# All gate and up products first, hidden values kept in DRAM, then all down products

## The chip, the cores and the metric

The kernel runs on one core of a Trainium2 chip. The time is the device time of the program in microseconds (us). Three timed runs of the kernel before gave 1355.43, 1355.92 and 1358.1 us, median 1355.92 us. The engines are named as the profile names them: PE (matmul), PEld (its weight load), DVE (vector), ACT (scalar), POOL (GpSimd) and SP (the queue that issues the DMAs).

## The reference, cut to what matters

```python
mod = (_silu(c) @ wmod).reshape(2, 6, 1, -1)          # shift, scale, gate of both halves
h = _layernorm(x) * (1 + ca) + sa                     # x: 2 batches x 2048 rows x 512
q, k, v = h @ q_w.T + q_b, h @ k_w.T + k_b, h @ v_w.T + v_b
qp, kp = elu(q) + 1, elu(k) + 1                       # 16 heads of 32
kv = einsum('bhsd,bhse->bhde', kp, v)
z = einsum('bhsd,bhd->bhs', qp, kp.sum(axis=2))
x = x + ga * ((einsum('bhsd,bhde->bhse', qp, kv) / (z + 1e-6)) @ o_w.T + o_b)
h = _layernorm(x) * (1 + cb) + sb
gate, up = h @ lut[gate_idx].T, h @ lut[up_idx].T     # 512 -> 1376; lut has 16 values
x = x + gb * ((silu(gate) * up) @ lut[down_idx].T)    # 1376 -> 512
```

All is float32. The kernel splits each operand of its large products into two float16 halves and makes three float16 matmuls of one float32 product (`three`, L1067 to L1075).

## The kernel before, in words

The 4096 rows are 8 groups of 512. Phase A takes the groups one after another: layer norm, transposes, 12 projections of 12 matmuls each (`out_a`: 4 of K, 4 of V, 4 of Q), the sum of the attention matrix (`kv_a`), and it stores the positive queries in DRAM. Phase B has 8 stages. Stage g makes the feed-forward half of group g and, between its pieces, the attention output of group g + 1.

The inner size of 1376 is 11 chunks `j` (the last has 96 rows). One item of phase B is one chunk of one group: gate product (12 matmuls), up product (12), then `silu(gate) * up` on ACT (L646) and DVE (`hid_full`, L1003), the split into halves on ACT (`hid_hi`, L652) and POOL (`hid_lo`, L485), and the down product (12 matmuls, 4 tiles of 3), which adds up in four PSUM banks over the 11 items. Gate and up have one PSUM bank each, so `up` of an item waits for `hid_full` of the item before.

The attention of group g + 1 goes through every engine. On PE: four `z_piece` (L1169, one in each of items 0 to 3), four `o_piece` (12 matmuls each; the first stands behind `up` and `down` of item 4), four `t_piece` (transposes, items 8 and 9). On DVE: after `hid_full` of items 0 to 3 one `qn_full` (reciprocal L941, product L943); then four `x1_tile` (L951 to L958). `o_piece(n, 0)` waits until `qn_lo` of POOL has ended for all four chunks (`qn_done`). POOL also adds the bias (`xob`, L430) between `qn_lo` 2 and 3.

The weights come as indices and are looked up by DVE (`look_step`, L807 to L830): a piece is 128 x 512 words and takes 19 steps (4 that take bits apart, 8 leaves L826, 7 picks L829). Two pieces at once make a wide unit, with the same 19 steps on 1024 words. There are 33 pieces (11 chunks x gate, up, down). Before, 29 of them are looked up in phase A, in stages of 5, 7, 7 (two groups each), 4, 3 and 3, and the last 4 in the first stage of phase B. A call of `lookup` spreads its steps over the slots of a stage; the order of each engine is the order in which the code is written. PE, DVE, ACT and POOL run the equal stages in hardware loops (`Fori`).

Of the kernel before, what the change touches and what calls it, by code (L numbers as in the profile page):

```python
# [34 lines left out]
P = 128  # L35
# [20 lines left out]
PARTS = 3  # L56
PIECES = FC * PARTS
LOOK_0, LOOK_PAIR, LOOK_5, LOOK_6, LOOK_7 = 5, 7, 4, 3, 3
LOOK_A = LOOK_0 + 2 * LOOK_PAIR + LOOK_5 + LOOK_6 + LOOK_7
LOOK_B0 = PIECES - LOOK_A  # L60

# [18 lines left out]
def adaln_kernel(nc, x, qwT, qb, kwT, kb, vwT, vb, owT, ob, lut, gateT, upT, downT, cT, wmod, out):  # L80
    with ExitStack() as ctx:
# [1270 lines left out]
```

## Time and profile before

| | |
|---|---|
| median of 3 runs | 1355.92 us |
| the profiled execution | 1356.93 us, of which the span is 1355.2 us |
| PE busy | 1203.5 us (89%) |
| DVE busy | 766.9 us (57%) |
| ACT, POOL busy | 422.2 us, 337.1 us |
| TensorE clock granted, mean | 0.951 |
| DMA | 63.86 MB, mean 47 GB/s |

The shares are averages over stages with different limits: phase A ends at about 521 us, and the rows by stage below keep them apart. A matmul's duration in the trace is longer than its distance from the next, since matmuls overlap; what a product costs is read from the starts.

### The profile page before, as it was taken

What the parts mean: (1) busy time and instruction counts of PE and PEld (TensorE: products, weight loads), DVE (VectorE), ACT (ScalarE), POOL (GpSimd) and SP (SyncE); (2) the same over time, 40 slices, a digit from 0 to 9 for tenths busy, and PEclk for the clock granted to TensorE, in tenths of its full rate; (3) what the DMA queues carried; (4) which work ended last, traced back from release to release, by engine and by line L of the source; (5) the groups of instructions that cost most, each with busy time, mean ns of one, the idle gap of its engine ahead of it and who ended that gap; (6) DMA issues with size and microseconds to landing.
All of it is one profiled execution on the core that took longest, in us unless ns stands there. A gap on an engine that the chain in (4) does not pass through costs nothing.

```text
span 1355.2 us, 14765 instructions
## 1 busy us (share of the span) xinstructions
PE 1203.5 (89%) x5464; PEld 582.6 (43%) x5464; DVE 766.9 (57%) x1073; ACT 422.2 (31%) x664; POOL 337.1 (25%) x338
## 2 busy tenths in 40 slices
PE   4587889978876757899999999999999999999998
PEld 4253345534433423344444444444444444444443
DVE  2479999999999766985833630531531531531111
ACT  0224446645534414113213213213213213212111
POOL 1120100000001013432522424324334334333212
PEclk9888899989988877899999999999999999999999
DMA  9225110111020102000200100100100100100000
GB/s 329 90 72 164 63 62 28 35 62 62 1 94 23 39 0 94 32 1 0 94 31 1 63 32 0 63 32 1 63 31 0 62 32 0 62 0 1 31 0 31
DMA packets 35455, 63.86 MB, mean 47 GB/s; under 512 B 3296, under 2 KB 13536, under 8 KB 33344
## 3 DMA queue, kind: packets, MB, share of 16 engines
q1 hardware_dynamic: 35392, 63.00, 13.7%
q8 instruction: 42, 0.69, 0.2%
q14 instruction: 21, 0.17, 0.0%
HBM read 46.22 MB, written 16.78 MB: 46 GB/s over the span
## 4 chain that ended last, share of the span: by engine, by line
PE 57%; DVE 29%; issue 9%; ACT 2%; POOL 2%; DMA 0%; POOLq 0%; ACTq 0%; DVEq 0%; SPq 0%
PE bank L1072 18%; PE bank L1073 18%; PE bank L1074 18%; DVE look_buf L829 6%; DVE look_buf L826 4%; DVE w_ffn L829 4%; PE bank L1169 2%; DVE arena L826 1%; DVE qn_f L941 1%; DVE shared L851 1%; DVE qp L859 1%; DVE look_buf L821 1%; DVE h L863 1%; PE bank L1080 1%; DVE shared L855 1%
## 5 line engine op out<-in xcount | busy, mean ns | idle before, releaser
L1072 PE MATMUL bank<-h,w_ffn 128*128 128x512 f16 (+1 forms) x704 | 269.2, 382 | 14.4 <-DVE hid_f L1003 6.1
L1074 PE MATMUL bank<-h,w_ffn 128*128 128x512 f16 (+1 forms) x704 | 269.3, 383 | 0.0
L1073 PE MATMUL bank<-h,w_ffn 128*128 128x512 f16 (+1 forms) x704 | 269.1, 382 | 0.0
L1003 DVE SCALAR_TENSOR_TENSOR hid_f<-bank,sc,shared 128x512 f32<-128x512 f32 (+1 forms) x88 | 65.9, 749 | 315.9 <-PE bank L1074 297.2
L485 POOL TENSOR_TENSOR shared<-hid_f,shared 128x512 f16<-128x512 f32 (+1 forms) x88 | 102.2, 1161 | 395.3 <-ACT shared L652 395.0
L646 ACT ACTIVATE shared<-bank,sc 128x512 f32<-128x512 f32 (+1 forms) x88 | 60.4, 686 | 273.2 <-PE bank L1074 273.2
L652 ACT ACTIVATE shared<-hid_f 128x512 f16<-128x512 f32 (+1 forms) x88 | 55.5, 631 | 281.9 <-DVE hid_f L1003 281.6
L1072 PE MATMUL bank<-w_ffn,shared 128*128 128x512 f16 (+1 forms) x352 | 137.1, 389 | 2.6 <-POOL shared L485 2.5
L1073 PE MATMUL bank<-w_ffn,shared 128*128 128x512 f16 (+1 forms) x352 | 137.0, 389 | 0.0
L1074 PE MATMUL bank<-w_ffn,shared 128*128 128x512 f16 (+1 forms) x352 | 136.6, 388 | 0.0
L1072 PE MATMUL bank<-arena,h 128*128 128x512 f16 x256 | 103.2, 403 | 12.6 <-DVE h L863 6.4
L1072 PEld LDWEIGHTS bank<-h,w_ffn 128*128 128x128 f16 (+1 forms) x704 | 71.0, 101 | 99.2 <-issue 14.9
L1073 PEld LDWEIGHTS bank<-h,w_ffn 128*128 128x128 f16 (+1 forms) x704 | 71.0, 101 | 86.4 <-issue 12.3
L941 DVE RECIPROCAL qn_f<-qn_f 128x512 f32<-128x512 f32 x32 | 107.0, 3343 | 1.8 <-ACT qn_f L598 1.8
L1074 PEld LDWEIGHTS bank<-h,w_ffn 128*128 128x128 f16 (+1 forms) x704 | 71.0, 101 | 82.9 <-issue 2.6
L1073 PE MATMUL bank<-arena,h 128*128 128x512 f16 x256 | 102.4, 400 | 0.0
L1074 PE MATMUL bank<-arena,h 128*128 128x512 f16 x256 | 101.5, 396 | 0.0
L1120 PE MATMUL bank<-shared 128*128 128x129 f32 x256 | 40.9, 309 | 50.9 <-DVE shared L855 50.9
L951 DVE SCALAR_TENSOR_TENSOR xg<-bank,sc,xg 128x512 f32<-128x512 f32 x32 | 24.0, 749 | 107.0 <-PE bank L1074 107.0
L396 POOL TENSOR_SCALAR ve<-mv 128x4 f32<-128x4 f32 x16 | 5.2, 326 | 315.8 <-DVE mv L739 211.4
L424 POOL TENSOR_TENSOR qn<-qn_f,qn 128x512 f16<-128x512 f32 x32 | 37.6, 1175 | 141.8 <-ACT qn L604 141.8
L526 ACT ACTIVATE h<-bank,modm 128x512 f16<-128x512 f32 x64 | 49.4, 773 | 53.6 <-PE bank L1080 27.6
(162 smaller groups left out, 1897.4 us busy)
## 6 DMA issues: line engine op xcount, KB each, us to landing
xg<-in_x SPq DMA_DIRECT2D x16, 1024.0 KB, 6.6
qp_dram<-qp SPq DMA_DIRECT2D x8, 1024.0 KB, 4.8
qp<-qp_dram SPq DMA_DIRECT2D x7, 1024.0 KB, 4.8
out<-xg SPq DMA_DIRECT2D x7, 1024.0 KB, 4.3
w_ffn<-in_wmod SPq DMA_DIRECT2D x5, 1024.0 KB, 14.3
w_ffn<-in_gateT SPq DMA_DIRECT2D x10, 256.0 KB, 4.5
w_ffn<-in_upT SPq DMA_DIRECT2D x10, 256.0 KB, 4.7
w_ffn<-in_downT SPq DMA_DIRECT2D x10, 256.0 KB, 5.1
```

What stands on the lines that cost most here:

```text
L485: pool.tensor_tensor(hid[0:m, i, 1], hid_f[0:m, i], hid[0:m, i, 0], ALU.subtract).then_inc(hid_done, 1)
L526: act.activation(h[:, par, 0, c], bank[c % 2][:], ACT.Identity, bias=bias, scale=scale)
L646: act.activation(silu_g[0:m, j % 2], bank[6][0:m], ACT.Silu, scale=c1(C_INV_G)[0:m]).then_inc(silu_g_done, 1)
L652: act.activation(hid[0:m, i, 0], hid_f[0:m, i], ACT.Copy).then_inc(hid_hi_done, 1)
L826: ins = dve.tensor_scalar(buf(dst), buf("m0"), tab_x[:, a:a + 1], tab[:, 2 * a:2 * a + 1], ALU.bitwise_and, ALU.bitwise_xor)
L829: ins = dve.copy_predicated(buf(dst), buf(a), buf(b))
L941: dve.reciprocal(qn_f[:, c % 2], qn_f[:, c % 2]).then_inc(rec_done, 1)
L1003: dve.scalar_tensor_tensor(hid_f[0:m, i], bank[7][0:m], c1(C_HID)[0:m], silu_g[0:m, i], ALU.mult, ALU.mult).then_inc(hid_f_done, 1)
L1072: pe.matmul(dst, a_hi, b_hi, start=first, stop=False)
L1073: pe.matmul(dst, a_hi, b_lo, start=False, stop=False)
L1074: last = pe.matmul(dst, a_lo, b_hi, start=False, stop=end)
L1120: last = pe.matmul(bank[6 + c // 2][:, at:at + n], kp[:, t % 2, c * P:(c + 1) * P], v_one[:, t % 2, c], start=(t == 0 and c % 2 == 0), sto ...
```

## The change: what it does, and the diff

- Phase B makes gate and up products only. The split hidden values of each item go to DRAM (`hid_dram`, 256 KB an item), through three buffers (`HIDS = 3`). A third phase C loads them group by group (two buffers of 11 chunks, laid over the gate and up weights, which are done with by then) and makes all down products, 33 items of three matmuls in one PSUM bank after the other. The rows `x` after attention go to DRAM (`x1_dram`) and come back in phase C.
- Gate and up have two PSUM banks each, so an item waits for the one two items back. The normed rows have three buffers (`H2S = 3`).
- The lookup goes in the order gate and up of all chunks, then down. Phase A does 16 pieces: one wide unit in each of groups 0 to 5, two single pieces in groups 6 and 7. Phase B does 17 single pieces: three in each of stages 0 to 4, two in stage 5. Stages 0, 1, 2 have 9, 11 and 13 items, since chunks 9 and 10 of groups 0 and 1 wait for their weights; the others have 11, and the last stage has no attention.
- The first stage of phase B has the attention pieces one or two items earlier than the others.
- The loops are written out.

```diff
-LOOK_0, LOOK_PAIR, LOOK_5, LOOK_6, LOOK_7 = 5, 7, 4, 3, 3
+HIDS = 3
+H2S = 3
+LOOK_A = [[(0, True)], [(2, True)], [(4, True)], [(6, True)], [(8, True)], [(10, True)],
+          [(12, False), (13, False)], [(14, False), (15, False)]]
+LOOK_B = [[(p, False) for p in range(a, b)] for a, b in ((16, 19), (19, 22), (22, 25), (25, 28), (28, 31), (31, PIECES))]
+HELD = FC - 2
+STAGES = [[(0, j) for j in range(HELD)],
+          [(1, j) for j in range(HELD)] + [(0, j) for j in range(HELD, FC)],
+          [(1, j) for j in range(HELD, FC)] + [(2, j) for j in range(FC)]]
+STAGES += [[(g, j) for j in range(FC)] for g in range(3, BATCHES * SEQ // GROUP)]
...
+            def hid_load(g):
+                par = g % 2
+                for s, count in landed(SLOT[(g, FC - 1)]):
+                    sp.wait_ge(s, count)
+                sp.dma_start(hid_all[par][:, 0:FC - 1]..., hid_dram[g][:, 0:FC - 1]).then_inc(hid_in[par], 16)
...
+                    sp.wait_ge(hid_done, e + 1)
+                    sp.dma_start(hid_dram[g][0:m, j], hid[0:m, e % HIDS]...).then_inc(hid_out[e % HIDS], 16)
...
             def hid_hi(e, j):
+                if e >= HIDS:
+                    act.wait_ge(hid_out[e % HIDS], 16 * (e // HIDS))
...
+                units = LOOK_B[s] if s < len(LOOK_B) else None
+                shares = HELD if s < 2 else len(STAGES[s])
+                for i, (g, j) in enumerate(STAGES[s]):
+                    if n < GROUPS:
+                        run(before, i)
+                    run(early, i)
+                    hid_full(SLOT[(g, j)], j)
+                    if n < GROUPS:
+                        run(after, i)
+                    run(extra, i)
+                    if units and i < shares:
+                        lookup(units, i, shares)
...
-                    up(g, par, j)
-                    if j:
-                        down(g, j - 1)
+            def up(g, j):
+                e = SLOT[(g, j)]
+                if e >= 2:
+                    pe.wait_ge(hid_f_done, e - 1)
+                gate_up(g, j, 1, bank[3 + 2 * (e % 2)]).then_inc(up_done, 1)
+
+            def down(g, t):
+                par, k = g % 2, 4 * g + t
+                if t == 0:
+                    pe.wait_ge(hid_in[par], 32 * (g // 2 + 1))
+                pe.wait_ge(y_read, k + 1)
+                ...
+                three(bank[2 + t][:], pairs).then_inc(sum_done, 1)
...
+            for s in range(2, GROUPS):
+                stage_b(s)
+            pe.wait_ge(hid_f_done, GROUPS * FC)
+            pe.wait_ge(down_ready, 1)
+            for g in range(GROUPS):
+                for t in range(TILES):
+                    down(g, t)
```

On DVE, one of the equal stages of phase B, items 0 to 3. Before:

```order
L1003 SCALAR_TENSOR_TENSOR hid_f<-bank,sc,shared 128x512
L941 RECIPROCAL qn_f<-qn_f 128x512
L943 SCALAR_TENSOR_TENSOR qn_f<-qp,qn_f 128x512
L1003 SCALAR_TENSOR_TENSOR hid_f<-bank,sc,shared 128x512
L941 RECIPROCAL qn_f<-qn_f 128x512
```

On DVE of the changed kernel, the same place in stage 3 (L1053 is `hid_full`, L994 and L996 `qn_full`, L878 to L886 lookup steps), from item 1 on:

```order
L1053 SCALAR_TENSOR_TENSOR hid_f<-bank,sc,shared 128x512
L994 RECIPROCAL qn_f<-qn_f 128x512
L996 SCALAR_TENSOR_TENSOR qn_f<-qp,qn_f 128x512
L883 TENSOR_SCALAR w_ffn<-look_buf,tab_x,tab 128x512
L883 TENSOR_SCALAR look_buf<-look_buf,tab_x,tab 128x512 x2
L886 COPY_PREDICATED w_ffn<-look_buf 128x512
L886 COPY_PREDICATED look_buf<-look_buf 128x512
L1053 SCALAR_TENSOR_TENSOR hid_f<-bank,sc,shared 128x512
L994 RECIPROCAL qn_f<-qn_f 128x512
L996 SCALAR_TENSOR_TENSOR qn_f<-qp,qn_f 128x512
```

Five lookup steps now stand between the product of one item and `hid_full` of the next.

On SP, one stage of phase B. Before (queries, output rows, input rows):

```order
L339 DMA qp<-qp_dram 128x2048
L346 DMA out<-xg 128x4x512
L349 DMA xg<-in_x 128x4x512
L353 DMA look_buf<-in_owT 128x4x512
L339 DMA qp<-qp_dram 128x2048
```

On SP of the changed kernel, one stage of phase B with its 11 stores of hidden values (L398):

```order
L369 DMA qp<-qp_dram 128x2048
L398 DMA hid_dram<-shared 128x1024 x3
L357 DMA x_dram<-xg 128x2048
L398 DMA hid_dram<-shared 128x1024 x2
L363 DMA xg<-in_x 128x4x512
L398 DMA hid_dram<-shared 128x1024
L398 DMA hid_dram<-shared 96x1024
L398 DMA hid_dram<-shared 128x1024 x4
L369 DMA qp<-qp_dram 128x2048
```

The store of the output has moved to phase C; the stores of hidden values and of `x` are new.

## Rows read from the trace of the kernel before

**Rows 1.** The page: busy time by engine; one group (busy us, mean ns | idle before)

```profile
PE 1203.5 (89%) x5464; PEld 582.6 (43%) x5464; DVE 766.9 (57%) x1073; ACT 422.2 (31%) x664; POOL 337.1 (25%) x338
...
L424 POOL TENSOR_TENSOR qn<-qn_f,qn 128x512 f16<-128x512 f32 x32 | 37.6, 1175 | 141.8 <-ACT qn L604 141.8
```

**Rows 2.** Busy time in windows, one a stage (columns are named in its first row)

```profile
core 0: us, PE busy (x) PEld busy (x) DVE busy (x) ACT busy (x) POOL busy (x), PEclk, DMA share, GB/s
73.70:140.70 67.00, 53.66 (x264) 31.23 (x263) 59.09 (x97) 27.50 (x43) 7.21 (x6) 0.90 0.42 119
140.70:192.00 51.30, 44.91 (x211) 22.82 (x210) 48.27 (x66) 25.92 (x41) 5.24 (x4) 0.90 0.12 42
192.00:233.70 41.70, 35.00 (x175) 18.97 (x174) 40.41 (x65) 24.45 (x39) 2.54 (x4) 0.92 0.15 51
...
323.70:378.10 54.40, 45.22 (x224) 23.39 (x222) 53.38 (x82) 25.84 (x41) 2.29 (x4) 0.97 0.12 39
378.10:437.60 59.50, 42.57 (x188) 21.68 (x188) 57.08 (x105) 25.13 (x40) 8.52 (x9) 0.86 0.15 53
437.60:521.40 83.80, 50.11 (x213) 24.66 (x214) 61.47 (x90) 31.13 (x51) 17.64 (x16) 0.78 0.17 63
521.40:636.90 115.50, 106.11 (x456) 47.59 (x457) 92.24 (x125) 28.25 (x44) 37.12 (x31) 0.94 0.03 10
636.90:747.40 110.50, 108.02 (x482) 49.50 (x481) 52.11 (x66) 26.75 (x42) 37.37 (x37) 0.98 0.11 39
...
849.70:952.00 102.30, 102.30 (x469) 47.10 (x468) 34.22 (x35) 26.76 (x42) 36.38 (x36) 1.00 0.09 32
...
1156.70:1259.00 102.30, 102.30 (x469) 47.13 (x468) 34.22 (x35) 24.31 (x38) 36.44 (x36) 1.00 0.06 21
```

**Rows 3.** Groups on DVE, 140.7 to 233.7 us: wide and single lookup steps

```profile
L829 DVE COPY_PREDICATED look_buf<-qn,arena 128x1024 uint32<-128x1024 uint32 x9 | 12.3, 1364 | 0.1
L826 DVE TENSOR_SCALAR look_buf<-arena,tab_x,tab 128x1024 uint32<-128x1024 uint32 x12 | 9.8, 816 | 0.1
...
L826 DVE TENSOR_SCALAR look_buf<-look_buf,tab_x,tab 128x512 uint32<-128x512 uint32 x7 | 3.6, 536 | 0.0
L829 DVE COPY_PREDICATED look_buf<-look_buf 128x512 uint32<-128x512 uint32 x4 | 3.0, 742 | 0.1
```

**Rows 4.** Timeline of PE in a full stage (start us, us, what)

```profile
952.02 0.38 PE L1072 MATMUL bank<-h,w_ffn 128*128 128x512 f16 x1
...
954.61 0.39 PE L1072 MATMUL bank<-w_ffn,shared 96*128 96x512 f16 x1
...
957.33 1.02 PE L1169 MATMUL bank<-qp,same_head 128*128 128x512 f32 x2
...
994.91 0.38 PE L1072 MATMUL bank<-arena,qn 128*128 x1
```

**Rows 5.** Timeline of DVE in the same stage, item 2

```profile
975.85 0.75 DVE L1003 SCALAR_TENSOR_TENSOR hid_f<-bank,sc,shared 128x512 f32<-128x512 f32 x1 [4.01 <-PE bank L1074]
...
979.89 0.69 DVE L943 SCALAR_TENSOR_TENSOR qn_f<-qp,qn_f 128x512 f32<-128x512 f32 x1
```

**Rows 6.** Timelines of DVE, POOL and PE in the first stage of phase B

```profile
555.25 1.81 DVE L829 COPY_PREDICATED w_ffn<-look_buf 128x512 uint32<-128x512 uint32 x1
...
558.64 2.88 DVE L826 TENSOR_SCALAR look_buf<-look_buf,tab_x,tab 128x512 uint32<-128x512 uint32 x2
...
555.00 6.23 POOL L430 TENSOR_TENSOR xg<-xg,obga 128x512 f32<-128x512 f32 x4
...
564.48 0.61 PE L1072 MATMUL bank<-h,w_ffn 128*128 128x512 f16 x1 [6.14 <-DVE hid_f L1003]
...
569.58 0.45 PE L1072 MATMUL bank<-w_ffn,shared 128*128 128x512 f16 x1
```

**Rows 7.** DMA issues: out<-in, KB each, us to landing

```profile
qp_dram<-qp SPq DMA_DIRECT2D x8, 1024.0 KB, 4.8
...
out<-xg SPq DMA_DIRECT2D x4, 256.0 KB, 2.0
```

More of the change, by code:

```diff
@@ L479, in _ @@
             for c in range(KC):
[L480 to L498 removed]
+                h_lo_b(0, c)
@@ L499, in stage_b, with m1_max @@
+            def m1_max():
+                pool.wait_ge(h2_done, 4 * 2 + 4 + 1)
+                all_max(S_M1, 8)
+            for s in range(GROUPS):
+                stage_b(s, {8: [m1_max]} if s == 1 else {})
+            for g in range(GROUPS):
+                par = g % 2
+                pool.wait_ge(x1_in[par], 16 * (g // 2 + 1))
                 for t in range(TILES):
@@ L830, in look_step, with lookup, looked @@
                 ins.then_inc(look, 1)
-            def in_twos(first, pieces):
-                return [(first + p, p + 1 < pieces) for p in range(0, pieces, 2)]
-            def lookup(units, before, share, shares):
-                total = len(units) * STEPS
-                if share == 0:
-                    dve.wait_ge(look, before)
-                    dve.sem_clear(look)
+            def lookup(units, share, shares):
+                first, total = UNITS.index(units[0]), len(units) * STEPS
                 for i in range(total * share // shares, total * (share + 1) // shares):
                     p, wide = units[i // STEPS]
-                    look_step(p, wide, i % STEPS, i // STEPS * STEPS)
+                    look_step(p, wide, i % STEPS, (first + i // STEPS) * STEPS)
+            def looked(unit, ready):
+                dve.wait_ge(look, (UNITS.index(unit) + 1) * STEPS)
+                dve.sem_inc(ready, 1)
             def k_bias(g, t):
@@ L870, in kv_sum, with stage_a @@
                     dve.tensor_tensor(acc, acc, kv_bank[i], ALU.add).then_inc(kv_read, 1)
-            def stage_a(g, par, more, look=None, extra={}, late=0):
+            def stage_a(g, par, more, units=None, extra={}, late=0):
                 if more:
@@ L887, in stage_a @@
                         kv_sum(g)
-                    if look:
-                        units, before, share, shares = look
-                        lookup(units, before, share + o, shares)
+                    if units:
+                        lookup(units, o, OUTS)
                 qp_sum(g, KC - 1)
@@ L983, in look_7 @@
                 for share in shares:
-                    lookup([(first_6 + LOOK_6 + p, False) for p in range(LOOK_7)], LOOK_6 * STEPS, share, OUTS)
+                    lookup(LOOK_A[7], share, OUTS)
             stage_a(7, 1, False, extra={
@@ L1007, in y_tile @@
                 k = 4 * g + t + 1
+                dve.wait_ge(sum_done, k)
                 dve.wait_ge(y_done, k + 2)
```

512 lines of the change are left out of this document (253 added, 259 removed).

## The prediction, made before the changed kernel had run

> **What bounds the kernel now.** First the page: PE is busy for 89% of the span, DVE for 57% [rows 1]. These are means over two kinds of stage, so next the windows by stage [rows 2]. In phase A (to 521.4 us) DVE is busy nearly always, 48.27 of 51.30 us or 40.41 of 41.70, and PE is not: DVE, with its lookups, sets the pace. From 849.7 us on a stage takes 102.3 us and PE is busy in all of it, DVE in 34.22: PE sets the pace. Last the timelines, for what a piece costs on each engine and how long the attention's way through DVE is.
>
> **PE's work in phases B and C.** The starts 952.02, 954.61 and 957.33 give 12 matmuls of a gate or up product 2.59 us and 12 of a down product 2.72 [rows 4]. A full stage is 11 x (5.18 + 2.72) = 86.9, so the attention's pieces on PE take 102.3 - 86.9 = 15.4. The change moves the down products and drops none: 88 x 7.90 + 7 x 15.4 = 803.0 us before and after. A stage of 11 items without down is 57.0 + 15.4 = 72.4 us; those of 9 and 13 items are 62.0 and 82.7.
>
> **Phase A: lookups leave DVE.** A wide step of the two common kinds takes 1.364 or 0.816 us, a single one 0.742 or 0.536 [rows 3]. Four bit steps (my estimate: 0.7 wide, 0.42 single), 8 leaves and 7 picks, less some 0.09 of overlap a step, make 17.2 us for a wide unit and 9.5 for a single piece. Group 0 loses one wide unit and a single one: 26.7 us of DVE. Groups 1 and 3 go from two wide units to one (17.2), 2 and 4 from a wide and a single one to one wide (9.4), 5 loses 17.2, 6 and 7 lose 9.5 each. That is 116 us, but PE's own work catches up: 12 projections of 2.59, the attention matrix and the transposes are some 36.5 us a group, and the last query sum of a group, the statistics and the first key product of the next stand in a row over three engines. I take 39.5 us for groups 1 to 4 (the 41.70 us stage, which has 40.41 of DVE work, is the nearest row; the floor is 36.5). So: group 0 from 67.0 to 53 (PE's columns and rows of the modulation stay), groups 1 to 4 from 183.0 to 158, group 5 from 54.4 to 41, group 6 from 59.5 to 50.5 (it stays DVE's: 57.08 busy), group 7 from 83.8 to 77, since its chain of reciprocals hardly has lookups in it [rows 2]. Sum: **68 us less**; bounds 45 (the chain over three engines holds each group at 43) and 82 (PE's floor everywhere).
>
> **Phase B: the attention's way no longer fits.** This is the term that decides. The first `o_piece` starts 994.91 - 952.02 = 42.9 us into a stage [rows 4], and five down products stand before it. Without them PE is there at 42.9 - 13.6 = 29.3 us. It needs all four chunks of `qn_full` and their halves. On DVE `hid_full` and `qn_full` of an item take 975.85 to 980.58, 4.7 us, and DVE waited 4.01 us for PE before it: DVE had room [rows 5]. Without lookups the fourth `hid_full` can start at 24.3 (four items of 5.18 and four of 0.86 on PE), its product ends at 29.0, the halves on POOL, 1.175 [rows 1], and on ACT, some 0.7 by the DVE product of that size [rows 5], end at 31: 2 us late. That is stage 6. In stages 3 and 4 three pieces are spread over 11 items, 5 steps behind each product, as the order of DVE shows. The chain is 6.1 (first `up`) + 3 x 4.7 + 15 steps (7.1) + 4.7 = 32.0, and what POOL costs.
>
> What POOL costs: in the first stage of phase B a single pick takes 1.81 us beside `xob` where it takes 0.742 alone, two leaves 2.88 instead of 1.0, and `xob` itself 6.23 [rows 6]. `qn_lo` and `xob` fall into just the three shares that count. I take 4.3 us a stage (a step held up by some 0.9 us twice, and two or three in the third share); bounds 1 and 8. The product then ends at 36.3, the halves at 38.3: PE waits 9 us. After a wait of this kind PE ran slowly: from 564.48 the 12 matmuls behind a wait of 6.14 us took 5.1 us to 569.58, at half the clock [rows 6], 2.5 us more. With 0.7 for the second chain (x1, norm, `t_piece`), which also has fewer PE products beside it, a stage loses 12.
>
> The Trainium skill has a rule on this in "SBUF — State Buffer", section "Who interferes with whom": DVE operations in a two-port mode or with two SBUF inputs and GpSimd operations exclude each other for a whole instruction, and the later one is fully blocked. By that rule all three pieces' steps of a stage are exposed to each of POOL's 31 operations, which speaks against moving them out of phase A, where POOL is nearly idle. The 1.81 us of the row agree with it. By it alone the loss of a stage would be nearer my upper bound, 8 us of POOL's cost, and the whole, with 3.7 more in six stages, near 1394 us.
>
> Stage by stage, what PE loses: stage 0 has 6.3 steps a share and its chain begins one item earlier, where PE is at 26: 15 of waiting, 2.5 of clock, and at the end the clamps of three rows and the last lookup stand before the halves of the next group, 5.5: 23. Stage 1 has 6.3 steps and the second attention matrix, for which DVE was busy 52.11 instead of 34.22 us [rows 2], partly in the chain, and POOL's maximum, for which DVE waits: 25. Stage 2, with what DVE brings along from there, 4.4 steps: 18. Stages 3 and 4: 12 each. Stage 5, two pieces, 3.5 steps: 10. Stage 6: 4. Stage 7: nothing. Together 104.
>
> Before, phase B took 1355.2 - 521.4 = 833.8, so 30.8 more than 803.0. Of these I keep 4 for the second matrix's products on PE and 4 for the end (last rows on DVE and POOL, and a DMA of 2.0 us [rows 7]); 23 go, and 104 + 1.5 (PE turns to phase C) come: **82.5 us more**. Two-deep banks are in this: they let PE run two items ahead of `hid_full`, but nothing lets it pass `o_piece`.
>
> **DRAM.** A store of 256 KB lands in 2.0 us, 1024 KB in 4.8 [rows 7]. The ring of three gives a store two items, 10 us: hidden, even behind a 1 MB transfer. A group's 2.75 MB in phase C need by the same row some 13 us, with output and input of 1 MB 23, beside 11 x 2.72 = 29.9 us of PE: hidden. The first load has the last four items (21 us) of stage 7. If loads ran at half that rate, phase C would show 16 us for each of six groups. Nothing there, 0 to 96 as bounds, with nearly all weight at 0.
>
> **Loops.** A stage in a loop and the last full one outside take 102.30 us alike [rows 2]: nothing. The Trainium skill ("Runtime: NRT & Kernel Launch", "Instruction fetch mechanics") says that a taken branch can stop the fetch and recommends unrolling; by it there would be a gain, which these two rows do not show.
>
> **Sum.** 1355.2 - 68 + 82.5 = 1369.7 of span, 1371.4 with the 1.7 us around it. The median of the runs is 1.0 under the profiled execution: 1370.5, rounded for the many small lags that were left out to **1372 us**.
>
> **Rivals.** (1) *Faster: the attention's way hides.* If POOL's operations fall beside the reciprocals, which do not use what lookups use, and DVE's queue is not in step with the items, stages 2 to 5 lose some 5 us, stages 0 and 1 some 12. Then 48 come instead of 104: 1316. For it speaks that DVE as a whole has time (34 + 29 of 72 us); against it that the shares stand before the next reciprocal in the same queue. (2) *Slower by much: DVE becomes the bound of stages 0 to 5.* In the first stage four pieces and a share raised DVE's busy time to 92.24 us. If a piece costs 13 us with POOL beside it, three make 39 and DVE's stage is 71 to 90 us with waits on top: stages lose 5 more each, 1400. It decides from some 12 us a piece. (3) *Slower: phase C waits for its loads,* 8 us for each of six groups on top of my forecast: 1420. Rows 7 speak against it. (4) *Phase A gains less,* 45: 1395; the 41.70 us stage speaks against it, since it is only 1.3 us longer than DVE's work. *Little changes:* the two terms are equal, within 3 us: only by accident.
>
> **Numbers.** A measurement of this kernel can tell 0.2%, 2.7 us, from no change. Forecast (1350 to 1392) 0.55, rival 1 0.22, rival 2 0.12, rival 3 0.03, rival 4 0.08. Of the forecast's own spread some 0.03 lies within 2.7 us of the time before and 0.02 below it, and rival 1 reaches up to it with 0.02: faster 0.22, same 0.05, slower 0.73. The range is 1328 to 1402; the likeliest case's own is 1352 to 1392.
>
> **What would show it.** Right: the first projections of phase B start at about 453 us; stages 1 to 4 of phase A take 38 to 41 us; in stages 2 to 5 of phase B the first matmul of `o_piece` has an idle time of 6 to 15 us in front of it, put down to POOL's `qn`, and half the clock behind it; phase C has PE busy throughout, 239 us. Wrong: stages 3 and 4 at 76 us or less, or waits in front of a group's first down product.

## The result, and the profile after

The changed kernel takes 1389.8 us (median of 4 runs, 1387.4 to 1391.8) against 1356.3 (4 runs, 1355.4 to 1358.1): ratio 1.0233, 95% interval 1.0214 to 1.0253. It is 33.5 us slower where 16 were forecast. The profiled execution took 1390.5 us, its span 1388.7. First the page, for [rows 1] and [rows 7]: busy time by engine, and DMA issues.

```profile
PE 1209.4 (87%) x5464; PEld 581.3 (42%) x5464; DVE 829.2 (60%) x1149; ACT 424.0 (31%) x664; POOL 356.8 (26%) x339
...
hid_dram<-shared SPq DMA_DIRECT2D x80, 256.0 KB, 2.0
w_ffn<-hid_dram SPq DMA_DIRECT2D x8, 2560.0 KB, 9.6
```

TensorE does the same 5464 matmuls; its busy time grows by 5.9 us (1203.5 before), since more of them run at the lower clock. The other 27.6 of the 33.5 us by which the span grew are idle time of TensorE. The windows tell where; for [rows 2], groups 0, 1, 2, 5 and 6 with 7 of phase A, then stages 0 to 7 of phase B and phase C.

```profile
72.20:126.20 54.00, 51.84 (x258) 30.58 (x257) 33.34 (x58) 27.27 (x43) 4.87 (x7) 0.87 0.46 138
126.20:170.60 44.40, 39.74 (x194) 20.77 (x193) 31.20 (x47) 25.41 (x40) 2.52 (x4) 0.92 0.14 48
170.60:207.10 36.50, 36.50 (x193) 19.69 (x192) 30.94 (x46) 25.41 (x40) 2.22 (x4) 1.00 0.17 58
280.20:322.50 42.30, 40.34 (x212) 21.66 (x211) 36.64 (x62) 25.95 (x41) 2.19 (x4) 1.00 0.15 51
322.50:455.00 132.50, 94.96 (x416) 47.91 (x414) 103.69 (x160) 56.55 (x91) 26.06 (x25) 0.84 0.18 62
...
455.10:543.00 87.90, 67.06 (x289) 30.12 (x290) 72.54 (x92) 25.40 (x40) 34.05 (x29) 0.89 0.28 102
543.00:655.50 112.50, 83.37 (x348) 38.28 (x349) 87.09 (x123) 26.07 (x41) 33.35 (x31) 0.85 0.15 52
655.50:753.20 97.70, 86.56 (x385) 40.44 (x384) 72.90 (x92) 29.45 (x46) 40.19 (x33) 0.95 0.18 64
753.20:839.70 86.50, 75.40 (x338) 34.84 (x337) 71.61 (x87) 26.70 (x42) 36.77 (x31) 0.94 0.21 72
839.70:927.20 87.50, 76.46 (x336) 35.19 (x336) 72.54 (x89) 26.69 (x42) 37.37 (x31) 0.94 0.19 69
927.20:1009.20 82.00, 74.96 (x336) 34.75 (x336) 59.91 (x72) 26.93 (x42) 36.32 (x31) 0.96 0.20 73
1009.20:1087.20 78.00, 74.37 (x337) 34.68 (x337) 34.12 (x35) 24.69 (x38) 31.97 (x31) 0.98 0.18 64
1087.20:1145.30 58.10, 57.20 (x266) 26.39 (x265) 9.00 (x12) 14.57 (x23) 12.71 (x11) 1.00 0.26 98
1145.30:1388.70 243.40, 238.78 (x1056) 100.88 (x1056) 24.02 (x32) 0.58 (x1) 42.11 (x33) 0.99 0.40 143
```

Phase A gives what it should: phase B starts at 455.1 instead of 521.4 us, 66.3 less. Groups 2 to 4 take 36.5 us, and PE is busy in all of it. Phases B and C take 933.6 instead of 833.8 us, 99.8 more, and C has no part in it: 243.4 us, PE busy for 238.8. Against the lengths of the prediction (62.0, 72.4, 82.7, four times 72.4, 57.0) the stages of B lose 25.8, 40.2, 15.0, 14.0, 15.1, 9.6, 5.6 and 1.0 us, 126.3 together; stage 1's contains some 4 us of the second M's products. "Lost" means this difference below.

Timeline of PE, stage 3, for the last of [rows 4] (start us, us, what [idle before <-releaser]):

```profile
791.10 0.59 PE L1116 MATMUL bank<-arena,qn 128*128 128x512 f16 x1 [8.36 <-issue]
...
795.96 0.38 PE L1116 MATMUL bank<-h,w_ffn 128*128 128x512 f16 x1
```

TensorE waits 8.36 us in front of the first `o_piece`, and its 12 matmuls take 4.86 us instead of 2.59. DVE's timeline, and then POOL's, say what it waits for, though the row names no engine ("issue"):

```profile
781.96 1.40 DVE L883 TENSOR_SCALAR look_buf<-look_buf,tab_x,tab 128x512 uint32<-128x512 uint32 x1
783.27 0.74 DVE L1053 SCALAR_TENSOR_TENSOR hid_f<-bank,sc,shared 128x512 f32<-128x512 f32 x1
783.94 3.34 DVE L994 RECIPROCAL qn_f<-qn_f 128x512 f32<-128x512 f32 x1
787.31 1.38 DVE L996 SCALAR_TENSOR_TENSOR qn_f<-qp,qn_f 128x512 f32<-128x512 f32 x1
```

POOL at the same time:

```profile
780.64 2.43 POOL L480 TENSOR_TENSOR qn<-qn_f,qn 128x512 f16<-128x512 f32 x1 [2.83 <-ACT qn L660]
783.03 5.11 POOL L486 TENSOR_TENSOR xg<-xg,obga 128x512 f32<-128x512 f32 x4
788.10 1.60 POOL L540 TENSOR_TENSOR shared<-hid_f,shared 128x512 f16<-128x512 f32 x1
789.66 1.33 POOL L480 TENSOR_TENSOR qn<-qn_f,qn 128x512 f16<-128x512 f32 x1
```

The fourth product ends at 788.69, 35.5 us into the stage (forecast 36.3), its low half on POOL at 790.99, and PE starts at 791.10. This is the forecast's mechanism.

Stage 1 has this wait too, 17.64 us, the longest of the phase. Behind it comes another, which was not forecast. Both on PE:

```profile
591.88 0.58 PE L1116 MATMUL bank<-arena,qn 128*128 128x512 f16 x1 [17.64 <-issue]
...
648.29 0.66 PE L1116 MATMUL bank<-h,w_ffn 128*96 128x512 f16 x1 [11.48 <-DVEq L899]
```

Then DVE, up to that moment:

```profile
630.72 0.77 DVE L1053 SCALAR_TENSOR_TENSOR hid_f<-bank,sc,shared 128x512 f32<-128x512 f32 x1
642.74 0.15 DVE L750 TENSOR_SCALAR sc<-sc 128x1 f32<-128x1 f32 x1 [11.25 <-POOL sc L446]
...
643.68 0.73 DVE L886 COPY_PREDICATED w_ffn<-look_buf 128x512 uint32<-128x512 uint32 x1
...
647.45 0.73 DVE L886 COPY_PREDICATED w_ffn<-look_buf 128x512 uint32<-128x512 uint32 x1
```

And POOL:

```profile
633.34 1.16 POOL L498 TENSOR_TENSOR arena<-h_f,arena 128x512 f16<-128x512 f32 x1
642.33 0.38 POOL L446 PARTITION_ALL_REDUCE sc<-sc  x1 [7.82 <-issue]
649.45 1.14 POOL L498 TENSOR_TENSOR arena<-h_f,arena 128x512 f16<-128x512 f32 x1 [6.75 <-issue]
```

DVE stands at `m_scale(1)` (L750) for 11.25 us, until POOL's maximum over the partitions is there. From the end of its operation before, POOL takes 8.2 us to it (7.82 put down to issue, 0.38 to the instruction), and 6.75 us more pass until its next operation, a low half of the next group's normed rows (L498, `h_lo_b`). Behind `m_scale` in DVE's queue stands the last share of stage 1's lookups, which completes piece 21, and gate (0,10) waits for that piece (L899 is `looked`). So TensorE waits for GpSimd's reduction, through a lookup that has nothing to do with it. DVE stood at the same place before the change, where it held nobody up (L693 is the same scale there):

```profile
733.71 0.15 DVE L693 TENSOR_SCALAR sc<-sc 128x1 f32<-128x1 f32 x1 [9.39 <-POOL sc L390]
```

### The profile page after: what moved, and what is told of

Its sections match the earlier page's. It is cut to its first block, busy times and chain, and to the rows that moved or that the text cites. A ratio compares the mean times of both kernels' runs of the same rounds, so it can differ in the third digit from the quotient of the medians.

```text
span 1388.7 us, 14324 instructions
## 1 busy us (share of the span) xinstructions
PE 1209.4 (87%) x5464; PEld 581.3 (42%) x5464; DVE 829.2 (60%) x1149; ACT 424.0 (31%) x664; POOL 356.8 (26%) x339
## 3 DMA queue, kind: packets, MB, share of 16 engines
q1 hardware_dynamic: 52160, 124.87, 25.8%
## 4 chain that ended last, share of the span: by engine, by line
PE 53%; issue 11%; DVE 6%; POOL 4%; ACT 1%; DMA 0%; POOLq 0%; DVEq 0%; SPq 0%; ACTq 0%
PE bank L1116 17%; PE bank L1117 16%; PE bank L1118 16%; PE bank L1213 2%; DVE look_buf L883 2%; POOL arena L493 1%; DVE look_buf L886 1%; POOL shared L540 1%; DVE w_ffn L886 1%; DVE hid_f L1053 1%; PE bank L1124 1%; PE bank L1203 0%; DMA h<-qp_dram 0%; POOL rstd L454 0%; PE bank L1164 0%
## 5 line engine op out<-in xcount | busy, mean ns | idle before, releaser
L1116 PE MATMUL bank<-h,w_ffn 128*128 128x512 f16 (+1 forms) x528 | 204.0, 386 | 23.8 <-DVEq L899 17.1
L1117 PE MATMUL bank<-h,w_ffn 128*128 128x512 f16 (+1 forms) x528 | 203.8, 386 | 0.0
L1118 PE MATMUL bank<-h,w_ffn 128*128 128x512 f16 (+1 forms) x528 | 203.2, 385 | 0.0
L540 POOL TENSOR_TENSOR shared<-hid_f,shared 128x512 f16<-128x512 f32 (+1 forms) x88 | 110.2, 1252 | 340.1 <-ACT shared L708 340.1
L1060 DVE SCALAR_TENSOR_TENSOR shared<-bank,sc,gb_row 128x512 f32<-128x512 f32 x32 | 24.0, 751 | 215.6 <-PE bank L1118 215.6
L1053 DVE SCALAR_TENSOR_TENSOR hid_f<-bank,sc,shared 128x512 f32<-128x512 f32 (+1 forms) x88 | 65.8, 748 | 138.3 <-PE bank L1118 106.5
L1116 PE MATMUL bank<-w_ffn 128*128 128x512 f16 (+1 forms) x352 | 136.3, 387 | 0.9 <-DVE hid_f L1053 0.9
L1117 PE MATMUL bank<-w_ffn 128*128 128x512 f16 (+1 forms) x352 | 136.2, 387 | 0.0
L1118 PE MATMUL bank<-w_ffn 128*128 128x512 f16 (+1 forms) x352 | 136.2, 387 | 0.0
L1116 PE MATMUL bank<-arena,qn 128*128 128x512 f16 x128 | 54.7, 427 | 74.6 <-issue 74.6
L1116 PE MATMUL bank<-arena,h 128*128 128x512 f16 x256 | 102.1, 399 | 11.5 <-issue 7.0
L883 DVE TENSOR_SCALAR look_buf<-look_buf,tab_x,tab 128x512 uint32<-128x512 uint32 x147 | 109.6, 777 | 0.8
L994 DVE RECIPROCAL qn_f<-qn_f 128x512 f32<-128x512 f32 x32 | 107.0, 3344 | 4.2 <-ACT qn_f L654 4.2
L701 ACT ACTIVATE shared<-bank,sc 128x512 f32<-128x512 f32 (+1 forms) x88 | 60.3, 685 | 115.2 <-PE bank L1118 115.1
L571 POOL TENSOR_TENSOR xg<-xg,shared 128x512 f32<-128x512 f32 x32 | 41.0, 1280 | 198.1 <-DVE shared L1060 198.1
L1116 PEld LDWEIGHTS bank<-h,w_ffn 128*128 128x128 f16 (+1 forms) x528 | 53.7, 102 | 89.0 <-issue 15.4
L1117 PEld LDWEIGHTS bank<-h,w_ffn 128*128 128x128 f16 (+1 forms) x528 | 53.7, 102 | 65.5 <-issue 11.3
L1118 PEld LDWEIGHTS bank<-h,w_ffn 128*128 128x128 f16 (+1 forms) x528 | 53.8, 102 | 63.4 <-issue 4.0
L480 POOL TENSOR_TENSOR qn<-qn_f,qn 128x512 f16<-128x512 f32 x32 | 45.6, 1424 | 120.3 <-ACT qn L660 120.3
## 6 DMA issues: line engine op xcount, KB each, us to landing
out<-xg SPq DMA_DIRECT2D x7, 1024.0 KB, 11.2
```

What stands on the lines that cost most here:

```text
L480: pool.tensor_tensor(qn[:, 1, c], qn_f[:, c % 2], qn[:, 0, c], ALU.subtract).then_inc(qn_done, 1)
L540: pool.tensor_tensor(hid[0:m, e % HIDS, 1], hid_f[0:m, e % 2], hid[0:m, e % HIDS, 0], ALU.subtract).then_inc(hid_done, 1)
L571: pool.tensor_tensor(xg[:, par, t], xg[:, par, t], y_t[:, t % 2], ALU.add).then_inc(y_done, 1)
L701: act.activation(silu_g[0:m, e % 2], bank[2 + 2 * (e % 2)][0:m], ACT.Silu, scale=c1(C_INV_G)[0:m]).then_inc(silu_g_done, 1)
L883: ins = dve.tensor_scalar(buf(dst), buf("m0"), tab_x[:, a:a + 1], tab[:, 2 * a:2 * a + 1], ALU.bitwise_and, ALU.bitwise_xor)
L994: dve.reciprocal(qn_f[:, c % 2], qn_f[:, c % 2]).then_inc(rec_done, 1)
```

## The experiments

Eleven kernels ran, each timed beside the kernel before; a ratio is to that one. The changed kernel is called "after" here. The kernel before took 1357.0 us beside experiments 1 to 4, 1358.0 beside 5 to 8 and 1360.2 beside 9 to 11, which ran on another chip than 1 to 8. Differences in microseconds to after, or between these sets, carry that drift of up to 4 us; the lengths of stages inside one execution do not. Two stages of the same code still differ by up to some 2.5 us: stage 0, whose program is that of after, lost 25.8 us there and 28.2 in experiment 4.

**1. No lookups in phase B.**

```
-                    if units and i < shares:
-                        lookup(units, i, shares)
...
-                            looked((p, False), gu_ready)
+                            dve.sem_inc(gu_ready, 1)
...
```

> The changed kernel without the 17 lookups of phase B (the weights of these pieces stay raw indices). Theory A (the lookups stand on DVE ahead of the reciprocals, and PE waits for them at the first o_piece): each of the stages 2 to 5 loses what stage 6 loses now, 5.6 us, instead of 15.0, 14.0, 15.1 and 9.6; stage 0 loses some 12 instead of 25.8, stage 1 some 16 instead of 40.2. Together 1390 - 69 = 1321 us. Theory B (with the down products gone the attention's way is too long for the stage even without lookups): waits of 6 to 8 us stay at each o_piece, 1355 us or more. Theory C (the traffic with DRAM holds phase B up): 1380 to 1390 us, no stage much shorter.

Measured 1333.2 us (ratio 0.981, 0.977 to 0.986): the lookups cost 56.6 us. The stages lose 13.2, 28.1, 7.1, 4.1, 5.8, 5.8, 5.8 and 1.0 us. Work is left out here, so 1333.2 is no time that a whole kernel could reach by this. The expected 1321 was missed by 12 us. Stage 1 loses 28.1 even so, and each later stage to stage 6 keeps a wait of 3.2 us in front of `o_piece`, where 2 had been worked out for stage 6:

```profile
751.75 0.38 PE L1114 MATMUL bank<-arena,qn 128*128 128x512 f16 x1 [3.19 <-issue]
```

In stage 1, 8.6 us of waiting are left at `o_piece` and 6.5 at gate (0,10). The second is the wait for POOL's maximum again: the signal that stands for piece 21 is still given behind `m_scale(1)`.

**2. All lookups, none of them beside the reciprocals.**

```
+                    first = 2 if s == 0 else 3
+                    k, parts = i - first, shares - first
+                    if units and 0 <= k < parts:
+                        lookup(units, k, parts)
...
```

> The same lookups, all of them, but in a stage's items 3 and later (2 and later in stage 0), behind the fourth reciprocal, none before. Theory A: the waits at o_piece shrink to some 3 us (as in stage 6) and stages 2 to 5 lose 6 to 8 us each instead of 13.4 in the mean; stage 0 gives back 8, stage 1 few, since its last share still stands behind POOL's maximum: 1350 to 1358 us. Rival (DVE's load as such is the bound, 34 us and three pieces in 72): the wait moves to the second half of the stage, before the transposes, and the time stays within 10 us of 1390.

Measured 1367.5 us (ratio 1.006, 1.003 to 1.008), 22 less than after with the same work. Stages 3 and 4 in windows:

```profile
742.40:824.50 82.10, 74.75 (x338) 34.73 (x337) 68.39 (x84) 26.85 (x42) 37.13 (x31) 0.98 0.20 74
824.50:906.60 82.10, 74.73 (x336) 34.74 (x336) 70.83 (x89) 26.53 (x42) 37.27 (x31) 0.98 0.20 73
```

DVE is nearly as busy as in after (68.4 and 70.8 us against 71.6 and 72.5) and the stages are 4 to 5 us shorter: of the 56.6 us that the lookups of phase B cost, some 22 are the price of where they stand. The other 34 stay, so their amount costs too. The waits at `o_piece` fall to 3.6 us (3.2 without lookups), and `t_piece` now waits 3.1 us for POOL's rows. The expected 1350 to 1358 was missed. Stage 0 gave back 2 us and not 8: `o_piece` waits 5.5 us instead of 11.9, but a gate now waits 2.6 us for its lookup, and the wait at the end grew from 6.6 to 7.8; stages 3 and 4 lost 9.7 and 9.8, not 6 to 8; and stage 1 gained 1.4 (38.8 us lost), for its wait for piece 21 grew to 13.6 us. The rival, a time within 10 us of 1390, is rejected too.

**3. `xob` at the start of a stage instead of in the chain.**

```
-                              3: [lambda: qn_lo(n, 2), lambda: xob(n, par)],
+                    before = {0: [lambda: xob(n, par)], ...
```

> Only POOL's adding of the bias (xob, four operations, 5.1 us) is moved in stages 1 to 6 from item 3 to item 0, where DVE waits for the first up product. Theory A with a share for POOL: the third lookup share is no longer held up and qn_lo(3) no longer stands behind xob, 1.5 to 3 us less in each of the six stages: 1373 to 1381 us. Rival (POOL's operations cost the lookups nothing that counts): 1390 us.

Measured 1395.8 us (ratio 1.027, 1.023 to 1.031): a miss, 6 us worse than after. Stage 1 loses 3.3 less, stages 2 to 5 lose 1.0 to 3.4 more each. `xob` now meets the share that the last item of the stage before left. DVE at the start of stage 3:

```profile
749.96 6.50 DVE L886 COPY_PREDICATED look_buf<-look_buf 128x512 uint32<-128x512 uint32 x1
756.49 0.73 DVE L886 COPY_PREDICATED look_buf<-look_buf 128x512 uint32<-128x512 uint32 x1
757.26 0.74 DVE L886 COPY_PREDICATED w_ffn<-look_buf 128x512 uint32<-128x512 uint32 x1
757.89 0.74 DVE L1053 SCALAR_TENSOR_TENSOR hid_f<-bank,sc,shared 128x512 f32<-128x512 f32 x1
```

POOL there:

```profile
749.76 1.19 POOL L540 TENSOR_TENSOR shared<-hid_f,shared 96x512 f16<-96x512 f32 x1 [2.77 <-ACT shared L708]
750.90 4.95 POOL L486 TENSOR_TENSOR xg<-xg,obga 128x512 f32<-128x512 f32 x4
```

One pick, 0.73 us alone like the one behind it, took 6.50 beside POOL's four additions, and the first reciprocal started 10.5 us into the stage. The contention is shown and is worse than forecast where it falls on a pick; the place for `xob` was wrong. The Trainium skill ("SBUF — State Buffer", "Who interferes with whom") has the later operation blocked for a whole instruction; here the pick, which had started 0.2 us after POOL's first operation in the rows (L540), ended only at 756.46, behind that operation and the whole run of four, which ended at 755.85.

**4. `m_scale(1)` one item later.**

```
-                        8: [lambda: m_scale(1)], 9: [lambda: m_cut(1, 0), lambda: m_cut(1, 1)],
+                        9: [lambda: m_scale(1), lambda: m_cut(1, 0)],
...
```

> Only the scale and the first cut of the second attention matrix are moved behind DVE's last lookup share of stage 1 (item 9 instead of 8). Theory D (the 11.5 us in which PE waits for gate product (0, 10) come from the last share of piece 21, which stands on DVE behind the wait for POOL's maximum): this wait goes, 8 to 11 us less, 1379 to 1382 us. Rival (DVE is late in stage 1 anyway): the wait turns up in stage 2 instead, and 3 us or less are won.

Measured 1386.8 us (ratio 1.020, 1.017 to 1.024), 3 us less: the wait goes, as theory D has it, but the time is the rival's. The wait of gate (0,10) falls from 11.5 to 0.9 us and stage 1 loses 26.6 instead of 40.2; stage 2 loses 26.0 instead of 15.0. The two stages together lose 52.6 instead of 55.2. So the cause of the wait is shown, and taking it away by itself wins little. Stage 2 takes it back in two places. Its first `o_piece` waits 13.4 us instead of 8.4, since the scale and the cuts now stand at the stages' border, and a new wait of 4.2 us comes near its start, which experiment 5 has too.

**5. M's scale and cuts in stage 2.**

```
-                        8: [lambda: m_scale(1)], 9: [lambda: m_cut(1, 0), lambda: m_cut(1, 1)],
-                        10: [lambda: m_cut(1, 2), lambda: m_cut(1, 3), lambda: dve.sem_inc(m_ready, 1)]},
+                stage_b(s, {8: [lambda: m_scale(1)], 9: [lambda: m_cut(1, 0)], 10: [lambda: m_cut(1, 1)],
+                            11: [lambda: m_cut(1, 2)], 12: [lambda: m_cut(1, 3), ...]} if s == 2 else {})
```

> The changed kernel with VectorE's scale and four cuts of the second batch's M moved out of stage 1 (items 8 to 10) into stage 2 (items 8 to 12); POOL's maximum stays where it is, and M is wanted only in stage 3. Nothing else moves. The theory that VectorE's queue stood behind the wait for POOL's maximum, and the lookup shares behind it: the wait of gate (0,10), 11.5 us, goes, and since neither scale nor cuts stand in stage 1 any more, stage 2 does not take it over as it did in the run with the scale one item later: stage 1 loses 24 to 29 us instead of 40.2, stage 2 stays at 14 to 17, and the time is 1374 to 1380 us. The rival, that the sum of VectorE's work in stages 1 and 2 decides and not the wait inside it (the cuts alone are some 8 us): stage 2 loses 8 us more than now, and the time is 1383 to 1388 us.

Measured 1382.8 us (ratio 1.018, 1.013 to 1.022): 7 less by the medians, between the two and next to the rival's 1383. The profiled execution was the slowest of the four (1387.2); in it phase B is 3.5 us shorter than in after. Stages 1 and 2:

```profile
543.10:643.10 100.00, 81.40 (x349) 37.47 (x350) 81.84 (x112) 23.89 (x38) 28.60 (x27) 0.88 0.15 56
643.10:746.70 103.60, 89.40 (x385) 41.45 (x384) 74.77 (x95) 30.82 (x49) 43.28 (x37) 0.92 0.18 63
```

Stage 1 loses 27.6 (12.6 less), stage 2 20.9 (5.9 more), stage 3 17.1 (3 more: its `o_piece` waits 11.4 us, since the cuts sit just before its first reciprocal). So of the 12.6 us that stage 1 gains, 9 come back by the windows. Stage 3's part is DVE's cuts. Stage 2's is not DVE's work, for DVE idles at the border for 14.5 us. Rows of PE, ACT and POOL show another way of the same reduction:

```profile
653.38 0.63 PE L1116 MATMUL bank<-h,w_ffn 128*96 128x512 f16 x1 [4.10 <-ACT shared L701]
...
651.22 0.78 ACT L582 ACTIVATE arena<-bank,modm 128x512 f16<-128x512 f32 x1 [11.82 <-POOL arena L498]
...
649.99 1.14 POOL L498 TENSOR_TENSOR arena<-h_f,arena 128x512 f16<-128x512 f32 x1 [6.94 <-issue]
```

POOL does nothing else from 635.2 to 650.0 us around its maximum. The low half of the normed rows (L498) stands behind it, ACT's next chunk of these rows waits for that, the silu of a gate (L701) stands behind it on ACT, and TensorE waits for the silu: 4.1 us and some 2.5 of clock. In after TensorE has no such wait there; the one of 11.5 us for the lookup lay over it.

**6. Late lookups, M in stage 2, the FFN gate rows clamped in stage 7.** The edits of 2 and 5, and `clamp(gb_row...)` moved from stage 0 to the stage without attention.

> Three moves on VectorE together, nothing left out: the lookups of phase B in items 3 and later of each stage (2 and later in stage 0), the scale and cuts of the second M in stage 2, and the clamps of the two FFN gate rows in stage 7, which has no attention, instead of stage 0. If the gains add: 1367.5 us of the run with late lookups, less the 13.6 us wait that stood in its stage 1, less 4 to 6 of the 7.75 us that gate (1,0) waited at the end of stage 0: 1346 to 1352 us. If a wait behind each takes half of it over: 1354 to 1360 us.

Measured 1364.9 us (10 runs; ratio 1.004, 1.002 to 1.007), 3 less than experiment 2, which is no more than the runs of either scatter: both expectations missed. Stage 1 gains the 13.3 us (38.8 to 25.5), but stage 3 loses 17.1 instead of 9.7 and stage 2 8.7 instead of 6.0; the clamps bring 1 us, since the last half on POOL, not DVE, ends stage 0. In stage 3 three late pieces and the cuts' heap meet: DVE is busy 76.40 us of it.

**7. The attention one pair later, with pairs held back in every stage.** The kernel of 6, and from stage 2 on:

```
+STAGES += [[(g - 1, j) for j in range(HELD, FC)] + [(g, j) for j in range(HELD)] for g in range(2, ...)]
+STAGES[-1] += [(BATCHES * SEQ // GROUP - 1, j) for j in range(HELD, FC)]
...
+                    if s >= 2:
+                        b_attn = {k + (k > 4): v for k, v in b_attn.items()}
+                        a_attn = {k + 1: v for k, v in a_attn.items()}
```

and the same shift on DVE, ACT, POOL and SP.

> The kernel of the run before in this call (late lookups, M's cuts in stage 2, clamps in stage 7), and from stage 2 on each stage begins with the last two gate/up pairs of the group before and holds its own last two back (stage 7 has 13 pairs), as stages 0 and 1 do already; the attention from o_piece to h_lo_b stands one pair later in these stages. The theory that what is left in stages 2 to 6 without lookups (5.8 us each: a wait of 3.2 us at the first o_piece for the chain of four reciprocals, and what the clock loses behind it) comes from where o_piece stands: TensorE reaches it 5.2 us later, the wait goes, t_piece has the same distance from o_piece, and two pairs stand between h_lo_b and the gate that needs it. Stages 2 to 6, which lost 6.0, 9.7, 9.8, 8.4 and 5.5 us with late lookups, lose 1 to 4 each: 20 to 30 us less than the run before in this call, 1318 to 1332 us, faster than both kernels. The rival, that the waits follow (t_piece 5 us, or the stage's end): within 6 us of the run before.

Measured 1340.8 us (ratio 0.987, 0.983 to 0.992): 24 less than the kernel of 6, as expected, and faster than both kernels; the expected 1318 to 1332 was missed because that kernel was slower than thought. Stages 2 to 6 lose 5.0, 11.6, 6.8, 2.4 and 0.8 us. The wait at `o_piece` is gone in all but stage 3 (4.1 us, behind the cuts), so the rest found in experiment 1 was the place of `o_piece`. What is left in these stages is mostly waiting at the first `t_piece` for POOL's rows, 2.1 to 4.8 us in stages 2 to 5.

**8. Every hidden value stored twice.**

```
+                    sp.dma_start(hid_twin[g][0:m, j], hid[0:m, e % HIDS]...).then_inc(hid_out[e % HIDS], 16)
```

> The changed kernel with each of the 88 stores of the hidden values done twice (256 KB once more, into a second DRAM tensor; each buffer comes free only when both have landed). It doubles what the DRAM passage costs, if it costs anything: by the theory that the stores are hidden (three buffers, 2.0 us a store against 5.2 us a pair) the time is the changed kernel's within 2 us, 1388 to 1392 us. If the passage through DRAM was part of the loss, by contention of the DMA queues or by buffers that come free late, it is 1395 us or more.

Measured 1388.6 us (ratio 1.021, 1.017 to 1.026), 1.2 less than after: no price, as expected. The stages' losses are those of after within 0.2 us, and the stores still land in 2.0 and 2.4 us:

```profile
hid_twin<-shared SPq DMA_DIRECT2D x80, 256.0 KB, 2.4
```

**9. After, with its 17 lookups dealt 3, 3, 1, 1, 2, 2, 2, 3 to eight stages.**

```
-LOOK_B = ... for a, b in ((16, 19), (19, 22), (22, 25), (25, 28), (28, 31), (31, PIECES))]
+LOOK_B = ... for a, b in ((16, 19), (19, 22), (22, 23), (23, 24), (24, 26), (26, 28), (28, 30), (30, PIECES))]
```

> The changed kernel with the 17 lookups of phase B dealt 3, 3, 1, 1, 2, 2, 2, 3 to the eight stages instead of 3, 3, 3, 3, 3, 2, 0, 0; nothing left out, nothing else moved. Against the run without any, the lookups cost stages 2 to 5 now 7.9, 9.9, 9.3 (three each) and 3.8 us (two). If a stage pays only for what goes beyond its slack (two cost 3.8, one costs nothing or 1, three in stage 7, which has no attention, nothing): 7, 9 and 5.5 us less in stages 2, 3 and 4, 4 more in stage 6: some 17 us less, 1370 to 1375 us. The rival, each lookup step at the same price wherever it stands: 3.3 us a lookup, so only the three that go to stage 7 are won: 10 us less, 1378 to 1382 us; if stage 7 pays too, 1388 us.

Measured 1378.9 us (ratio 1.014, 1.011 to 1.017): 11 less by the medians, 13 by the ratios. The time lies in the rival's range; the stages decide against it. Stages 2 to 7 lose 4.9, 6.2, 9.4, 9.5, 9.5 and 5.8. For the price of a lookup stage by stage: against the run without any, one makes stage 2 shorter by 2.2 us and stage 3 longer by 2.1. Both come mostly from the clock behind `o_piece` (12 matmuls in 2.59 us against 5.07, and in 3.87 against 2.59), so one costs next to nothing; two cost 3.6 to 3.8, three 7.9 to 9.9 (stages 2 to 4 of after). The price rises, as the first expectation had it, but stage 7 was not free: the last piece stands in front of phase C, whose first matmul waits 5.6 us for it.

**10. The kernel of 7 with that deal.**

> The skewed kernel (late lookups, M's cuts in stage 2, clamps in stage 7, pairs held back in every stage) with the lookups dealt 3, 3, 1, 1, 2, 2, 2, 3. Its stages lost 5.0, 11.6, 6.8, 2.4, 0.8 and 1.0 us from stage 2 on. Stage 3 lost 4.1 us at the first o_piece behind VectorE's cuts of M and lookups, and 3.6 at the first transpose. If VectorE's backlog set these: 6 to 12 us less, 1329 to 1335 us. If not (the transposes wait for POOL's rows in any case): within 3 us of 1340.8, and stage 6 up to 2 us longer.

Measured 1332.7 us (ratio 0.979, 0.976 to 0.981), 8 us less than experiment 7 as expected, and the fastest kernel of the study. Stages 2 to 4:

```profile
639.40:713.90 74.50, 72.75 (x337) 34.46 (x336) 50.37 (x59) 27.07 (x43) 36.48 (x33) 1.00 0.22 75
713.90:788.60 74.70, 72.73 (x338) 34.49 (x337) 48.89 (x57) 26.39 (x42) 34.27 (x31) 1.00 0.23 80
788.60:863.40 74.80, 72.75 (x338) 34.48 (x337) 57.73 (x67) 26.84 (x42) 35.55 (x31) 1.00 0.23 81
```

They take 74.5 to 74.8 us where TensorE's own work is 72.4, at the full clock. What is left stands above all in stage 0 (21.0 us), stage 1 (27.0) and in front of phase C (5.6).

**11. After without the lookups of phase A.**

> The changed kernel without the lookups of phase A (its first 16 pieces stay indices: work left out, the outputs are not the reference's); those of phase B stay. The prediction priced phase A's gain from VectorE to TensorE: groups 1 to 4 went from some 52 us to TensorE's own time. If TensorE bounds them in the changed kernel (36.5 of 36.5 us busy in groups 2 to 4), they stay at 36.5 us, and only group 5 (42.3), the last group (which shares VectorE with the first attention) and the start gain: phase B starts 5 to 15 us earlier than 455.1, and the time is 1375 to 1385 us. If VectorE still set the groups, each would be 3 us or more shorter than 36.5 us and phase B start before 435 us: 1370 us or less.

Work is left out here too. Measured 1360.9 us (ratio 1.0005, 0.999 to 1.002): phase B starts at 427.0, 28 us earlier than in after. For the windows of phase A above, groups 1, 2, 5 and 6 with 7:

```profile
126.00:165.20 39.20, 36.58 (x193) 19.84 (x192) 14.41 (x27) 25.11 (x40) 1.65 (x4) 1.00 0.16 54
165.20:201.70 36.50, 36.50 (x195) 19.82 (x193) 14.54 (x28) 25.11 (x40) 1.59 (x4) 1.00 0.17 58
274.40:311.90 37.50, 37.00 (x198) 20.12 (x196) 20.06 (x44) 25.23 (x40) 1.75 (x4) 1.00 0.17 57
311.90:427.00 115.10, 93.58 (x436) 47.76 (x435) 61.20 (x84) 54.77 (x88) 23.19 (x25) 0.90 0.18 66
```

With DVE's work halved, groups 2 to 4 stay at 36.5 us: TensorE bounds them, as expected. But DVE still costs 5 us each in groups 1 and 5 and 17.5 in groups 6 and 7, so phase B starts 28 us earlier instead of 5 to 15. The time is one that the second expectation allowed, but its cause, groups shorter than 36.5 us, did not come. One lookup fewer in each of groups 6 and 7 was not the end of DVE's bound there.

## Why the prediction was half right

Direction, mechanism and range held: the time lies in the likeliest case's own range. The size did not: 16 us is the difference of two terms of 68 and 82.5, and stages that lose 18 us more than the 104 forecast are enough to double it. The span is 19.0 us over the forecast 1369.7, and the windows split that: 1.7 from phase A, 18.3 from phase B's stages, 1.5 less than forecast in phase C with its end; the rest is rounding in the sum.

**Phase A, 68 us: right, by errors that cancel.** 66.3 measured. Groups 2 to 4 took 36.5 us, the floor and not 39.5: there is no chain over three engines to pay for. Group 1 took 44.4, groups 6 and 7 132.5 instead of 127.5 together; experiment 11 shows the lookups on DVE behind both: without them these groups take 39.2 and 115.1. None of groups 1 to 4 took the 38 to 41 us that were named as a sign.

**The attention's way, stages 2 to 6: right.** Forecast 18, 12, 12, 10, 4; measured 15.0, 14.0, 15.1, 9.6, 5.6. The three parts of the price are each seen: lookups in the chain (experiment 2 takes them out of it and the waits fall from 8.4 to 3.6), POOL's contention (the rows at 781.96 and 787.31 above take 1.4 us where 0.54 and 0.69 are the time alone, and experiment 3; no run gives what it costs within the chain), the lower clock (12 matmuls in 4.2 to 4.9 us). The term for stage 6, a bare chain 2 us late, was 3.2 us late; with the clock and 0.5 at `t_piece` 5.6. That stages 3 and 4 lost 2 to 3 more than forecast is mostly `t_piece`, which waits 2.6 us for POOL's rows where 0.7 was allowed with the second chain. Against the signs, the waits in stages 2 to 4 are 8.4 us and in stage 5 5.7, just under the 6 named, and the profile puts them down to "issue", not to POOL's `qn`.

**The step that failed: stage 1, "the second attention matrix ... partly in the chain, and POOL's maximum, for which DVE waits: 25".** With the 4 us of M's products that is 29; it measured 40.2, and 11.2 of the 18.3 us are here. The wait for the maximum was seen but priced as delay of DVE's chain only. What the runs put in its place: behind the waiting `m_scale` stood the lookup of a piece that TensorE needed in the same stage, so the wait passed to TensorE whole, 11.5 us and 2 of clock, on top of the 17.6 us at `o_piece`. Experiment 4 removes that wait and the stage loses 26.6, experiment 5 27.6, where 29 were forecast. Before the change the same wait was there, 9.4 us, but every piece had been looked up by then (29 in phase A, four in stage 0), and nothing behind it was wanted soon. The rule for an added wait, to name what is queued behind it and who waits for that, applied to a wait that was old, since the change put something new behind it.

This places the miss, and does not make the wait worth 11 us. With it gone, stages 1 to 3 still lose 66.6 (experiment 4) and 65.6 us (experiment 5), against 69.2 in after and 59 forecast, M's 4 us included. The forecast let POOL's maximum hold up DVE alone. But POOL does nothing else for 15 us around it, and TensorE pays for that by a second way too, through POOL's low halves and ACT.

**Stage 0, 23: 25.8.** The wait at `o_piece` was 11.9 us (15 forecast), and 6.6 at the end (5.5) were named; unnamed were 2.3 us at `t_piece` and what the clock took at the start of the stage, where 12 matmuls took 3.9 us.

**DRAM, 0: right; loops, 0: not tested by itself.** Experiment 8 doubles the stores at no cost. The 96 us that the upper bound held did not come: phase C has PE busy for 238.78 of 243.40 us. No run puts the loops back.

**Rivals.** (1) had stages 2 to 5 lose some 5 us each; they lost 9.6 to 15.1: rejected. (2) DVE as the bound: DVE is busy 72 of 87 us in stages 3 and 4, and experiment 2 shortens the stage with the same DVE work, so rejected there; in stage 3 of experiment 6, with M's cuts on top, it comes near. (3) rejected by phase C. (4) did not happen: phase A gave 66.3 us, not 45.

**What stays open.** Stage 1 loses 27 us in the best kernel. There it waits 8.6 us at `o_piece`, 2.2 at M's products and 3.4 at gate (0,10), with the lower clock behind these and at its start, and it holds M's own 4 us; no run took these apart, and none moved POOL's maximum. Nor did a run separate, within the 9 us of three pieces, DVE's plain queueing from POOL's contention.

## What to carry to other kernels

When work moves to a queue that has an old wait in it, look for what now stands behind that wait and which engine needs it next: a wait that cost nothing becomes one of the pacing engine's. Look also for every other way from the same cause, since with one wait gone the next may show (experiments 4 and 5 won back a fraction of the 11.5 us). When filler work leaves a stage (here 13.6 us of down products before `o_piece`), the chain it covered keeps its length, so the consumer must move by what the chain is then late: without lookups in it 3.2 us, for which one pair of 5.2 us was enough. Shifting the attention by one pair, holding two pairs over the border, keeping the first three items of DVE's queue free of filler, moving M's cuts and dealing the lookups evenly turned a loss of 2.3% into a gain of 2.1%. Deal filler evenly over the stages: its price in a stage rises faster than its amount.

## What the hardware showed that was not expected

- One pick on DVE that takes 0.73 us alone took 6.50 us beside POOL (experiment 3). It started beside one POOL operation and ended 0.6 us after the last of the four additions that followed: it was held for the whole run, not for one operation.
- After a wait TensorE's clock did not fall in step with the wait's length. Twelve matmuls take 2.59 us at the full clock. Behind waits of 0.7 to 2.6 us in front of gate products they took 2.6 us; behind waits of 3.2 to 3.6 us at `o_piece` anything from 2.59 to 5.08 us; behind 4 to 18 us at either 3.9 to 5.2 us.
- A maximum over the partitions of one column, 0.38 us in the profile, came 8.2 us after the end of POOL's operation before (6.3 in the kernel before), and the next operation started 6.75 us after it (7.05). The profile calls both gaps issue, so POOL does not look busy.
